# Router logits in column quadrants with their transpose, a 128-row selector for the gate bias, and a shifted position table in an attention and mixture-of-experts kernel

## The reference

```python
def _L0_gnn_ref(x, adj, Wq, Wk, Wv, Wg, bg):           # 8 heads of 32
    q, k, v = ...                                       # x @ Wq.T, x @ Wk.T, x @ Wv.T by heads
    scores = jnp.einsum('bqhd,bkhd->bhqk', q, k) / jnp.sqrt(jnp.float32(DK))
    attn = jax.nn.softmax(jnp.where(mask, scores, -jnp.inf), axis=-1)
    c = jnp.einsum('bhqk,bkhd->bqhd', attn, v).reshape(b, n, h)
    gate = jax.nn.sigmoid(jnp.concatenate([c, x], axis=2) @ Wg.T + bg)
    return gate * x + (1.0 - gate) * c

def _L0_ffn_ref(x, router_w, Wg, Wu, Wd, Sg, Su, Sd):  # 8 experts, the best 2 of each token
    full_scores = jax.nn.softmax(flat @ router_w, axis=-1)
    w, idx = jax.lax.top_k(full_scores, K)
    ...                                                 # weighted expert outputs, and a shared expert

x = x + _L0_gnn_ref(_layernorm(x), adj, ...)
x = x + _L0_ffn_ref(_layernorm(x), ...)
```

## Time and profile before

| | |
|---|---|
| median of 3 executions | 1997.55 us (1993.05 to 1998.07) |
| the profiled execution's own time | 1996.57 us |
| its span, first to last instruction | 1994.8 us |
| TensorE busy | 1798.7 us, 90% |
| VectorE busy | 1336.1 us, 67% |
| ScalarE busy | 1099.8 us, 55% |
| GpSimd busy | 955.7 us, 48% |
| mean granted TensorE clock | 0.97 of full speed |

### The profile page before, as it was taken

The page is one execution under the profiler, slowest core; times in us unless marked ns, Lnnn a source line. Parts: engine busy times, 40 slices in busy tenths (PEclk is TensorE's granted clock), DMA queues, the critical chain, the costliest instruction groups (busy, mean ns, idle before and its releaser), DMA issues.

```text
span 1994.8 us, 36000 instructions
## 1 busy us (share of the span) xinstructions
PE 1798.7 (90%) x12597; PEld 1502.8 (75%) x12597; DVE 1336.1 (67%) x3032; ACT 1099.8 (55%) x2489; POOL 955.7 (48%) x632
## 2 busy tenths in 40 slices
PE   5899999999999999999569999999999999999887
PEld 4677777777777777777458888888888888888776
DVE  5567767767776776776365444567777877787674
ACT  4878777877777788777123333333333433333332
POOL 1124443334444333443345000267777877777666
PEclk8999999999999999999779999999999999999999
DMA  5444455544455544543245222355555555455453
GB/s 151 118 130 113 145 159 154 144 139 141 132 153 160 154 139 146 147 131 103 75 146 188 90 89 93 137 170 136 140 154 154 152 138 138 135 154 154 117 138 43
DMA packets 141329, 269.20 MB, mean 135 GB/s; under 512 B 15456, under 2 KB 92640, under 8 KB 136160
## 3 DMA queue, kind: packets, MB, share of 16 engines
q1 hardware_dynamic: 112608, 226.19, 36.7%
q0 software_dynamic: 28128, 39.93, 9.9%
q10 hardware_dynamic: 416, 0.79, 0.2%
HBM read 141.99 MB, written 74.52 MB: 109 GB/s over the span
## 4 chain that ended last, share of the span: by engine, by line
PE 26%; POOL 10%; issue 8%; DMA 4%; DVE 1%; SPq 1%; ACT 0%; DVEq 0%; POOLq 0%
PE fbank L1269 8%; PE fbank L1270 8%; PE fbank L1271 8%; POOL out_x L1155 6%; POOL wl L1124 4%; DMA xb<-xg_dram 3%; PE fbank L1264 1%; DMA out_x<-yb,ix 0%; DVE xl L1411 0%; DVE am L1421 0%; ACT ah L1363 0%; DMA raw<-in_w_all 0%; SPq L1193 0%; DVE wh L1395 0%; DVE wa L1451 0%
## 5 line engine op out<-in xcount | busy, mean ns | idle before, releaser
L792 DVE CUSTOM_DVE_ANT_0 pf<-bank,bias_q 128x512 f32<-128x512 f32 x512 | 350.8, 688 | 270.8 <-PE bank L439 261.5
L1124 POOL TENSOR_TENSOR wl<-raw,wh 128x1024 fp32r<-128x1024 f32 x120 | 310.5, 2760 | 330.5 <-DVE wh L1395 330.5
L1424 DVE TENSOR_TENSOR al<-am,ah 128x512 fp32r<-128x512 f32 (+1 forms) x220 | 329.0, 1496 | 147.7 <-ACT ah L1363 147.7
L568 ACT ACTIVATE pf<-pf,nmax 128x512 f32<-128x512 f32 x512 | 373.6, 730 | 47.0 <-DVE nmax L792 44.9
L1363 ACT ACTIVATE ah<-am 128x512 fp32r<-128x512 f32 (+1 forms) x220 | 133.1, 605 | 412.4 <-DVE am L1421 412.4
L1269 PE MATMUL fbank<-xh,wh 128*128 128x512 f32 (+1 forms) x880 | 336.1, 382 | 19.9 <-DVE xl L1411 12.9
L1270 PE MATMUL fbank<-xl,wh 128*128 128x512 f32 (+1 forms) x880 | 335.4, 381 | 0.0
L1271 PE MATMUL fbank<-xh,wl 128*128 128x512 f32 (+1 forms) x880 | 335.2, 381 | 0.0
L449 PE MATMUL bank<-ident,pf 128*128 128x128 f32 x2048 | 315.1, 277 | 18.4 <-ACT pt L556 18.2
L556 ACT ACTIVATE pt<-bank 128x512 f32<-128x512 f32 x512 | 307.5, 601 | 15.9 <-PE bank L449 15.4
L449 PEld LDWEIGHTS bank<-ident,pf 128*128 128x128 f32 x2048 | 256.7, 142 | 74.8 <-issue 23.9
(11 more groups left out here) (207 smaller groups left out, 3298.5 us busy)
## 6 DMA issues: line engine op xcount, KB each, us to landing
raw<-in_w_all SPq DMA_DIRECT2D x39, 1536.0 KB, 8.6
stack<-qk SPq DMA_DIRECT2D x378, 128.0 KB, 2.3
xb<-xg_dram SPq DMA_DIRECT2D x32, 520.0 KB, 4.2
adj_i<-in_adj SPq DMA_DIRECT2D x32, 512.0 KB, 5.4
xn<-in_x SPq DMA_DIRECT2D x16, 512.0 KB, 5.2
xn_dram<-xn SPq DMA_DIRECT2D x16, 512.0 KB, 3.1
xp<-in_x SPq DMA_DIRECT2D x16, 512.0 KB, 6.2
xnp<-xn_dram SPq DMA_DIRECT2D x16, 512.0 KB, 7.2
```

The costliest lines, as they stand in the source:

```text
L568: act.activation(pf[i][:, :], pf[i][:, :], ACT.Exp, bias=nmax[:, i:i + 1], scale=-1.0, accum_out=den[:, g, tq, j:j + 1]).then_inc(p_exp, 1)
L792: dve.tensor_tensor_reduce(pf[r][:, :], S[p % 2][:, :], bias_q[1 - par][:, tq, :], -SCALE, -3.0 * MASKED, ALU.add, ALU.min, nmax[:, r:r + ...
L1124: pool.tensor_tensor(wl[s][:, c], raw[s][:, c], f32(wh[s][:, c]), ALU.subtract).then_inc(s_wl, 1)
L1424: dve.tensor_tensor(al[s][:, m, 0:cols], am[m % 2][:, 0:cols], f32(ah[s][:, m, 0:cols]), ALU.subtract).then_inc(s_al, 1)
```

## The change

A new unit M0 is put behind L0. L0 is one piece now, at position 0: the router weights, widened with zeros from 8 to 32 columns (`rw_wide`), are the stationary operand, and the four token tiles go through them into four column groups of 32, so that the bank holds logits by expert. ScalarE copies them to `lgt` (128x128), M0 at position 1 turns them back with one transpose, and ScalarE copies the 4 x 8 columns that count to `lg`. X0 and X1 go from positions 29 and 30 to 28 and 29. With M0 there are 19 units, and banks are counted over batches. choose, mark and weigh go from VectorE's positions 3, 4 and 6 to 4, 5 and 7, ScalarE's exp of the second choice from 5 to 6. The bias product has 128 rows: `pick2` holds ones in rows 0 and 1 and zeros below.

```diff
-UNIT_AT = {"L0": 0, "Q1": 2, "K1": 4, "V0": 6, "V1": 8, "C0": 10, "C1": 11, "R0": 12, "Z0": 14, "Z1": 15, "Z2": 16,
-           "Z3": 17, "P0": 18, "P1": 19, "Q0": 22, "K0": 24, "X0": 29, "X1": 30}
-HALVES = "LQKV"
-
-ACT_AT = {"exp": 5}
-DVE_AT = {"choose": 3, "mark": 4, "weigh": 6, "place": 14, "stat": 8, "var": 9, "bias0": 11, "bias1": 16, "gate": 19,
+UNIT_AT = {"L0": 0, "M0": 1, "Q1": 2, "K1": 4, "V0": 6, "V1": 8, "C0": 10, "C1": 11, "R0": 12, "Z0": 14, "Z1": 15, "Z2": 16,
+           "Z3": 17, "P0": 18, "P1": 19, "Q0": 22, "K0": 24, "X0": 28, "X1": 29}
+HALVES = "QKV"
+
+ACT_AT = {"exp": 6}
+DVE_AT = {"choose": 4, "mark": 5, "weigh": 7, "place": 14, "stat": 8, "var": 9, "bias0": 11, "bias1": 16, "gate": 19,
...
-        def bank(par, name):
-            return G[ORDER.index(name) % 3]
+        def bank(b, name):
+            return G[unit(b, name) % 3]
...
-                    pe.matmul(o[:, 0:D], ones2[0:2, :], bg2[0:2, :], start=True, stop=False)
+                    pe.matmul(o[:, 0:D], pick2[:, :], bg2[:, :], start=True, stop=False)
...
-                    for i in (2 * piece, 2 * piece + 1):
-                        for kf in range(KF):
-                            last = pe.matmul(o[:, E * i:E * i + E], zt[:, N * kf + P * i:N * kf + P * i + P],
-                                             rw[:, kf, :], start=kf == 0, stop=kf == KF - 1)
+                    for kf in range(KF):
+                        for i in range(NT):
+                            last = pe.matmul(o[DK * i:DK * i + DK, 0:P], rw_wide[:, kf, :],
+                                             zt[:, N * kf + P * i:N * kf + P * i + P], start=kf == 0, stop=kf == KF - 1)
+                elif name[0] == "M":
+                    pe.wait_ge(g_free, unit(b, "L0") + 1)
+                    last = pe.transpose(o[:, 0:P], lgt[:, :], ident[:, :])
...
                 elif name[0] == "L":
+                    act.wait_ge(g_full, unit(b - 1, "M0") + 1)
+                    act.activation(lgt[:, :], o[:, 0:P], ACT.Copy).then_inc(g_free, 1)
+                elif name[0] == "M":
                     act.wait_ge(s_rt, (b - 2) * RT)
-                    act.activation(lg[:, :, :], o[:, 0:NT * E].rearrange("p (i e) -> p i e", e=E),
+                    act.activation(lg[:, :, :], o[:, 0:P].rearrange("p (i c) -> p i c", c=DK)[:, :, 0:E],
                                    ACT.Copy).then_inc(g_free, 1)
...
-            dve.memset(f32(ones2[:, :]), 1.0).then_inc(s_set, 1)
+            dve.memset(f32(pick2[:, :]), 0.0).then_inc(s_pick, 1)
+            dve.wait_ge(s_pick, 1)
+            dve.memset(f32(pick2[0:2, :]), 1.0).then_inc(s_set, 1)
+            dve.memset(rw_wide[:, :, :], 0.0).then_inc(s_pick, 1)
...
+                dve.wait_ge(s_pick, 2)
+                dve.tensor_copy(rw_wide[:, :, 0:E], rw[:, :, :]).then_inc(s_pick, 1)
...
-                dve.wait_ge(g_free, unit(A + 2, "L0") + 1)
+                dve.wait_ge(g_free, unit(A + 2, "M0") + 1)
```

More of the change, by code:

```diff
@@ L108, in attention_phase @@
         bg2 = sb("bg2", [P, D], F32R)
-        ones2 = sb("ones2", [P, P], F32R)
+        pick2 = sb("pick2", [P, P], F32R)
         rw = sb("rw", [P, KF, E])
+        rw_wide = sb("rw_wide", [P, KF, DK])
+        lgt = sb("lgt", [P, P])
         ident_b = sb("ident_b", [P, P], BF16)
@@ L176, in attention_phase @@
         s_half = sem("s_half")
+        s_pick = sem("s_pick")
         s_held_pe, s_held_dve, s_held_pool, s_held_sp = (sem(f"s_held_{e}") for e in ("pe", "dve", "pool", "sp"))
@@ L221, in has @@
             kind = name[0]
-            return (late(b) if kind in "RL" else att if kind == "V" or name in ("Q1", "K1") else
+            return (late(b) if kind in "RLM" else att if kind == "V" or name in ("Q1", "K1") else
                     post if kind in "CZX" else pre)
@@ L364, in do_unit @@
                 B, A = b + 1, b - 1
-                o = bank(par, name)
+                o = bank(b, name)
                 k = int(name[1])
@@ L492, in evacuate @@
                 B, A = b + 1, b - 1
-                o = bank(par, name)
+                o = bank(b, name)
                 k = int(name[1])
                 act.wait_ge(g_full, unit(b, name) + 1)
-                if name[0] in "ZL":
+                if name[0] in "ZLM":
                     act.wait_ge(g_free, unit(b, name))
@@ L617, in prepare @@
                 dve.wait_ge(s_rt0, 4)
+                dve.wait_ge(s_pick, 3)
                 dve.nop().then_inc(s_set, 2)
```

## The result

The changed kernel takes 2053.72 us (median of 4 runs, 2051.47 to 2064.36); the kernel before, run beside it, 1995.3 (4 runs, 1992.51 to 1998.07). The ratio is 1.0303, 95% interval 1.0263 to 1.0343: slower, inside the range, 8 us under the predicted time.

The account below looks back on a forecast made before the run. It saw TensorE bound at the gate products, VectorE at positions 8 to 12, and clock falls at the seam. -20.5 + 6.8 - 11.8 + 12.8 + 54.6 + 3.3 + 21 = +66 us on 1996.6 gave 2062; range 2012 to 2090.

Parts of the forecast that it names:

- The large term: Positions 7 to 12: GpSimd holds the moved weighing, TensorE's score product S(12) 3.9 us late, +54.6; clock falls there, +21.
- The drain: After the last batch: the same hold delays the split of ct and so Z0, +3.3 us.
- rival 1: Position 7: the hold ends with GpSimd's first operation, VectorE's D(10) 1.45 us late; 2015 us in all, chance 0.09.
- The line 694 addition: Between VectorE's D(9) and D(10): its 1.2 us hold beside x1 would be over by then, leaving 0.17 us throughout.
- the wait on D(8): Before S(10): TensorE waits near 4 us for D(8), VectorE's mask-and-maximum of position 8.
- the lower clock: Positions 10 to 13: granted clock at its lower level in most batches, charged 1.5 us each, +21 us.
- S(12) would still wait for D(10): Position 12: TensorE's score product waits for VectorE's mask-and-maximum of position 10, so nothing hides its 3.9 us lateness.
- Bias: Gate products, positions 14 to 17: 128 rows save 0.36 us in Z1 to Z3 and 0.20 in Z0, -20.5 us.
- +0.45 us a seam: Between batches, S(28) to the next S(4): the new logits and X0's wait for xn2 together, 15 times, +6.8 us.
- I take 8 falls in 15: Seam, behind X0's new 1.5 us idle stretch: 8 clock falls of 1.6 us in 15 seams, +12.8 us.
- The rival that L0's column groups don't overlap: Seam: L0 costs 1.7 us as before, M0 and S(2) a further 1 us late, 15 times; 2077 us, chance 0.08.
- the rival without hold: Position 7: the weighing isn't held, so the terms of hold and clock drop out; 1984 us, chance 0.15.

Follow-up runs that it names:

- weigh_alone: The kernel before with only the weighing moved from VectorE's position 6 to 7 and its exp from 5 to 6: 2083.28 us, ratio 1.041.
- weigh_back: The changed kernel with the weighing back at VectorE's position 6 and its exp at 5: 1993.41 us, ratio 0.998 to the kernel before.
- two_ops_ahead: The changed kernel with the weighing's copy and token-number addition moved to the end of mark, position 5: 2014.98 us, ratio 1.0078 to the kernel before.
- weigh_ahead: The changed kernel with the weighing still in position 7, but ahead of c_tok instead of behind it: 2025.24 us, ratio 1.0128 to the kernel before.
- before_var10: The kernel before with the next batch's variance (line 694) at VectorE's position 10 instead of 9: 1997.48 us, ratio 0.9992.
- weigh_x_back: The changed kernel with weighing back at 6, exp at 5, and X0 and X1 back at 29 and 30: 1959.35 us, ratio 0.9805 to the kernel before.

## Why the prediction was right, and where it wasn't

**The large term was right, and is shown.** Moving the weighing behind c_tok makes it meet GpSimd's two operations on 128x1024, the subtraction and the x1 addition. weigh_alone loses 4.1% by it alone, and weigh_back, without it, loses nothing. The hold and its clock had +54.6 and +21, together 75.6; the 14 stretches S(9) to S(14) show 76.7. How the 76.7 divide between hold and clock isn't shown, as none of them is at full clock. The drain had +3.3. There the hold does make TensorE wait that much longer for ct_l, first before, then changed:

```profile
965.90 0.35 PE L397 MATMUL bank<-bg,ones 2*128 2x256 f32 x1 [1.54 <-DVE ct_l L656]
...
1025.07 0.55 PE L400 MATMUL bank<-bg,pick 128*128 128x256 f32 x1 [4.76 <-DVE ct_l L671]
```

But counted from the last S(31) this product starts no later (15.62 us, 15.74 before), as the new L0 and the absence of a clock fall save as much ahead of it. The prediction had no term for that.

**How VectorE is held was put wrongly.** The prediction let the multiplication alone stand through both GpSimd operations, from the row of 5.89 us in the earlier trace rows. In the trace the copy stands beside the first and the multiplication beside the second, and two_ops_ahead shows that with one such operation the hold ends with GpSimd's first: rival 1's mechanism. I had given rival 1 a chance of 0.09. The sum still came out because there are two operations that can be held for two that hold, and that is luck: where only one such operation stands there, as in two_ops_ahead, the same reasoning says no change from 2053.72, and the time is 2014.98. I hadn't counted the copy as one of them, since it has a single SBUF input. The earlier trace rows could have warned me: the addition of line 694 has a single SBUF input too, and was held. The Trainium skill has both points in "SBUF — State Buffer", section "Who interferes with whom": the second to issue blocks until the first finishes, and copies can contend too, in a two-port mode. By the first point the trace agrees (2.15 us beside 2.37); whether this copy is in such a mode no run shows, only that it was held for 2.15 us. Set against the Trainium skill's rule stood one row of the expert phase; that row is no exception there, but that phase has the other kind too. In the timeline of the kernel before, an al subtraction that begins 1.8 us into a run of two GpSimd operations ends 2.2 us ahead of the run's end:

```profile
1520.81 1.47 DVE L1424 TENSOR_TENSOR al<-am,ah 128x512 fp32r<-128x512 f32 x1 [0.70 <-ACT ah L1363]
```

the run being 1519.00 to 1524.53. Of the 33 al subtractions in that trace that meet the first of two or three GpSimd operations in a row, 24 take 4.36 us or more and end 0.56 us behind the last of the row, and 9 take 1.5 us. The 9 all begin 1.8 us into GpSimd's first operation; 23 of the 24 begin between 0.11 us ahead of it and 1.53 us into it. What decides between them was not tried, nor why no VectorE operation of the attention phase stood through two.

**The line 694 addition** went to 0.17, as said, and the wait on D(8) (3.93 us) and the lower clock (below 1.00 in 14 of 14 batches) came as said. That S(12) would still wait for D(10) did not: it waits for nothing.

**Bias: the term was right, its worth less.** -20.5 predicted, -20.6 by the positions. Done alone it brings 16.5 us (1998.65 - 1982.16); in the trace some of it comes back as clock falls elsewhere.

**Seam: the structure was right, the count of falls not.** +0.45 us a seam predicted and 0.45 measured (13.44 against 12.99), with X0's wait at 1.57 us (1.5 predicted). In that agreement two errors cancel: L0 starts 0.36 us later behind S(28) than predicted (9.04 us against 493.1 - 484.42 = 8.68) and takes 0.6 instead of 1.0. The falls at positions 0 to 3 are gone, as said; those that are left stand at position 28. The term that was mis-sized is "I take 8 falls in 15": there were 5, four of them in the 14 seams above and one in the seam ahead of them, each of about the 1.6 us predicted. That is 5 of the 8 us by which the prediction is too high. In weigh_back, with the same code at the seam, there are 9 in 14, four of them double. So the size of a fall can be read from a trace of before, and their number can't be read from the code of the seam. Each count is from one traced execution; the mean granted clock of the 17 executions of the kernel before that ran beside weigh_back goes from 0.961 to 0.970, so the number is likely to change from one execution to the next as well. The rival that L0's column groups don't overlap is out: 0.65 us for 16 passes.

**The 1984 us of the rival without hold was wrong as well.** weigh_back is that case on the chip: 1993.41. And weigh_ahead shows how little it takes: S(12) is 0.6 us later there, and the time is 31.8 us longer (2025.24 - 1993.41).

## What to carry to other kernels

An operation of four elements can be the costliest of a position if it stands beside GpSimd's long ones: look at what GpSimd is released to do by the instruction just ahead of it, and put such operations ahead of that instruction, or in another position. A product that waits for another engine belongs behind the group that can cover the wait, in the program as well as in the slot. And of a change with several parts, time each part: here two that gain 2% together (logits and bias) came with two that lose more (the weighing 4.1% alone, the earlier X0 1.7% beside the new logits, though 0.4% alone).

## What the runs showed that I had not expected

- The clock can turn a small lateness into a large one. weigh_ahead: S(12) 0.6 us later, falls in 10 of 14 batches, 31.8 us more time. before_var10: 0.7 us a batch gained at full clock, 0.3 in the mean, nothing that shows in the time.
- The number of falls in a seam is 4, 9 and 0 of 14 in the changed kernel, in weigh_back and in weigh_x_back: the first two have the same code at the seam and differ in where the weighing stands, some 20 positions earlier.
- A VectorE copy with one SBUF input took 2.15 us instead of 0.17 beside a GpSimd subtraction.
- Sixteen passes in four column groups with 128 moving columns take 0.65 us, 0.04 us a pass.
